# Unused products in two stages' waits, and normalisation statistics taken beside the last attention additions

## The reference

```python
x = x + L0_attn_a(ln(x))   # 16 heads, one shared key and value head, no mask
x = x + L0_ffn(ln(x))      # one 128x128 product, both sides quantised to a 6-bit grid per block of 32
x = x + L0_attn_b(ln(x))   # 16 heads of 64, causal
x = x + L0_ffn(ln(x))
x = x + L1_attn_a(ln(x))   # causal, keys and values from a latent of 32 columns
x = x + L1_ffn(ln(x))      # 8 experts, top 2 by softmax router, plus a shared expert
x = x + L1_attn_b(ln(x))   # causal, with biases
x = x + L1_ffn(ln(x))
```

## Time and profile before

| | us |
|---|---|
| median of 3 runs | 2551.67 |
| lowest, highest | 2545.71, 2552.09 |
| profiled execution | 2546.37 |
| its span, first to last instruction | 2544.7 |
| norm stage, from its first to its last work | 1370.3 to 1408.0 |
| latent attention | 1408.8 to 1791.1 |
| first expert stage's head, to the first gate product | 1792.0 to 1805.1 |
| second expert stage's head, to the first gate product | 2461.1 to 2474.2 |

### The profile page before, as it was taken

One profiled execution on the slowest core, in us unless ns is written; L12 is line 12 of the kernel. 1 busy time (PEld: TensorE's weight loads), 2 busy tenths in 40 slices (PEclk: granted clock), 3 DMA queues, 4 the chain that ended last, 5 costly groups with the idle time before them and its releaser, 6 DMA issues. The chain is left out here.

```text
span 2544.7 us, 48765 instructions
## 1 busy us (share of the span) xinstructions
PE 2449.8 (96%) x20081; PEld 1284.8 (50%) x20081; DVE 1509.0 (59%) x2063; ACT 1216.4 (48%) x1827; POOL 1246.4 (49%) x812
## 2 busy tenths in 40 slices
PE   7999999999999999999997999999989999999989
PEld 4444444444444455545554666666554555455545
DVE  5666656786555664556654567675554555555544
ACT  4544445544545555455542345445334554455541
POOL 4877778777766564555544000000015555555530
PEclk9999999999999999999997899999999999999999
DMA  3000000000000000000001100000000000000000
GB/s 85 1 1 1 1 1 1 1 1 1 1 1 1 1 1 1 1 1 1 1 1 23 35 3 3 3 3 3 1 1 1 1 1 1 1 1 1 1 1 17
DMA packets 18657, 13.04 MB, mean 5 GB/s; under 512 B 3074, under 2 KB 17795, under 8 KB 18308
## 3 DMA queue, kind: packets, MB, share of 16 engines
q1 hardware_dynamic: 18436, 9.92, 1.5%
HBM read 8.87 MB, written 1.05 MB: 4 GB/s over the span
## 5 line engine op out<-in xcount | busy, mean ns | idle before, releaser
L1542 POOL TENSOR_TENSOR sums<-sums,p 128x1024 f32<-128x1024 f32 (+3 forms) x384 | 817.7, 2129 | 370.5 <-PE ps L1169 326.4
L1364 DVE TENSOR_REDUCE half_max<-ps 128x2 f32<-128x1024 f32 (+3 forms) x384 | 442.1, 1153 | 382.3 <-PE ps L1148 344.1
L1261 ACT ACTIVATE p<-ps 128x1024 f32<-128x1024 f32 (+3 forms) x384 | 347.7, 916 | 229.8 <-PE ps L1125 170.4
L1122 PE MATMUL ps<-q,k 64*128 64x512 f32 (+3 forms) x1792 | 428.1, 556 | 0.0
L880 POOL TENSOR_TENSOR sums<-sums,p 128x1024 f32<-128x1024 f32 (+3 forms) x160 | 277.4, 1733 | 187.4 <-PE ps L627 171.1
L1169 PE MATMUL ps<-p,v 128*64 128x512 f32 (+3 forms) x1536 | 338.5, 555 | 0.0
L1125 PE MATMUL ps<-max_row,pick 64*128 64x512 f32 (+3 forms) x896 | 326.3, 725 | 0.0
L779 DVE TENSOR_REDUCE half_max<-ps 128x2 f32<-128x1024 f32 (+3 forms) x128 | 130.1, 1019 | 154.8 <-PE ps L606 121.4
L1148 PE MATMUL ps<-k_near,q_near 64*128 64x512 f32 (+2 forms) x896 | 195.8, 434 | 21.6 <-DVE half_max L1364 19.6
L1785 ACT ACTIVATE p<-ps 128x2048 f32<-128x2048 f32 (+1 forms) x80 | 136.5, 1707 | 163.0 <-PE ps L1681 91.5
L1148 PEld LDWEIGHTS ps<-k_near,q_near 64*128 64x128 f32 x896 | 84.6, 186 | 224.4 <-issue 124.8
(11 more groups left out here) (290 smaller groups left out, 3955.2 us busy)
## 6 DMA issues: line engine op xcount, KB each, us to landing
q_w<-in_wq SPq DMA_DIRECT2D x3, 512.0 KB, 5.4
o_w<-in_wo SPq DMA_DIRECT2D x3, 512.0 KB, 7.7
x<-in_x SPq DMA_DIRECT2D x4, 256.0 KB, 3.8
k_w<-in_wk SPq DMA_DIRECT2D x2, 512.0 KB, 6.8
v_w<-in_wv SPq DMA_DIRECT2D x2, 512.0 KB, 7.5
out<-x SPq DMA_DIRECT2D x4, 256.0 KB, 2.3
p<-in_wq_t SPq DMA_DIRECT2D x1, 512.0 KB, 5.2
p<-in_w_out SPq DMA_DIRECT2D x1, 512.0 KB, 7.2
```

The costliest lines, as they stand in the source:

```text
L1122: nc.tensor.matmul(out[:, head, 0:width], a.k[rows, owner(i) % 3, k * P:(k + 1) * P], a.q[rows, i % 3, s * BANK + lo:(s + 1) * BANK], star ...
L1261: act.activation(probabilities(g)[:, :, lo:BANK], score[g % 2][:, :, 0:BANK - lo], ACT.Exp)\
L1364: last = v.tensor_reduce(out, chunk_ps(c)[:, :, 0:hi - lo], AX.X, ALU.max, negate=True)
L1542: pool.tensor_tensor(sums, sums, probabilities(g)[:, :, lo:BANK], ALU.add).then_inc(summed, 1)
```

## The change

Unused products on TensorE: 60 (`2 * WARM`) at the norm stage's start, before the wait for the weight loads; 30 after the wait for the copied weights; the 30 that stood there before keep their place. In latent attention 15 (`WARM // 2`) stand before chunk 0, at step -6. They are 128x128 products of the identity. At the head of both expert stages the six unused products of 512 columns become four.

Statistics: `m.stats` is now one buffer that outlives the phases. In latent and in biased attention, DVE measures the tiles that it has just added to, for the last two items (i >= ITEMS - B), after a wait for its own addition. These are the last additions into each tile. The expert stages no longer measure at their head. The measuring at the end of the first expert stage, for the layernorm behind it, uses the same buffer.

```diff
--- before.py
+++ after.py
@@ -324,6 +324,12 @@
                     last = nc.tensor.transpose(m.ps[:, 4 + g, t * P:(t + 1) * P], xn[:, g * TPG + t, :], m.ident[:])
                 last.then_inc(turned, 1)
 
+            def keep_busy(times):
+
+                for _ in range(times):
+                    nc.tensor.matmul(m.ps[:, 4, 0:P], m.ident[:], m.ident[:], start=True, stop=True)
+
+            keep_busy(2 * WARM)
             pe.wait_ge(latent_in, 4 * 16)
             for h in range(H):
                 last = nc.tensor.matmul(m.ps[:, 0, h * LATENT:(h + 1) * LATENT], wq_t[:, h, :], k_up_t[:, h, :],
@@ -335,6 +341,7 @@
                                         start=True, stop=True)
             last.then_inc(latent_mm, 1)
             pe.wait_ge(latent_copied, 2)
+            keep_busy(WARM)
             if linear:
                 for pair in groups[::2]:
                     for g in (pair, pair + 1):
@@ -348,8 +355,7 @@
                             last = nc.tensor.matmul(m.ps[:, g, t * P:(t + 1) * P], m.xn_t[:, at:at + P],
                                                     m.ffn_wt[:], start=False, stop=t == TPG - 1)
                         last.then_inc(product, 1)
-                for n in range(WARM):
-                    nc.tensor.matmul(m.ps[:, 0, 0:P], m.ident[:], m.ident[:], start=True, stop=True)
+                keep_busy(WARM)
             for g in groups:
                 pe.wait_ge(normed[g % 2], normed_by(int(linear), g))
                 turn(g)
@@ -826,6 +832,10 @@
                 at = i % B * QT + s * TPG
                 x = m.x[:, at:at + TPG, :]
                 v.tensor_tensor(x, x, small.rearrange("p (t d) -> p t d", d=D), ALU.add).then_inc(small_out, 1)
+                if i >= ITEMS - B:
+                    dve.wait_ge(small_out, n + 1)
+                    for t in range(at, at + TPG):
+                        v.bn_stats(m.stats[:, t, :], m.x[:, t, :])
 
             if biased:
                 v.tensor_scalar(a.qk_bias[:, :, 0:1], a.qk_bias[:, :, 0:1], SCALE, None, ALU.mult)\
@@ -1764,6 +1774,9 @@
 
             for g in range(FIRST, END):
                 ahead, behind = chunks_at(g)
+                if 0 in ahead:
+                    for _ in range(WARM // 2):
+                        nc.tensor.matmul(score[:, 0, 0:P], m.ident[:], m.ident[:], start=True, stop=True)
                 for c in ahead:
                     chunk(c)
                 if 0 <= g < TOTAL:
@@ -1862,6 +1875,10 @@
                 at = i % B * (S // P) + 2 * s
                 x = m.x[:, at:at + 2, :]
                 v.tensor_tensor(x, x, small[:, 0:QW].rearrange("p (t d) -> p t d", d=D), ALU.add).then_inc(small_out, 1)
+                if i >= ITEMS - B:
+                    dve.wait_ge(small_out, n + 1)
+                    for t in (at, at + 1):
+                        v.bn_stats(m.stats[:, t, :], m.x[:, t, :])
 
             v.memset(a.neg_max[:], 0.0).then_inc(cleared, 1)
             dve.wait_ge(cleared, 1)
@@ -1928,7 +1945,7 @@
         gated, upped, spread = sem("gated"), sem("upped"), sem("spread")
         silued, hidden, downed, summed_out = sem("silued"), sem("hidden"), sem("downed"), sem("summed_out")
         first_mul, coef_low, stored = sem("first_mul"), sem("coef_low"), sem("stored")
-        stats, mv = sb("stats", [P, TILES, 6]), sb("mv", [P, TILES, 2])
+        stats, mv = m.stats, sb("mv", [P, TILES, 2])
         var, rstd, shift = (sb(name, [P, TILES]) for name in ("var", "rstd", "shift"))
         logit, prob, coef, rank = (sb(x, [P, TILES, EXPERTS]) for x in ("logit", "prob", "coef", "rank"))
         red = sb("red", [P, TILES])
@@ -2035,7 +2052,7 @@
                 for _ in range(times):
                     nc.tensor.matmul(m.ps[:, bank, :], m.ident[:], m.gate[:, 0:BANK], start=True, stop=True)
 
-            keep_busy(0, 6)
+            keep_busy(0, 4)
             turn(0, 0)
             for g in range(1, GROUPS):
                 turn(0, g)
@@ -2179,8 +2196,6 @@
                 x = m.x[:, g * TPG:(g + 1) * TPG, :]
                 v.tensor_tensor(x, x, m.ps[:, 6, :].rearrange("p (t d) -> p t d", d=D), ALU.add).then_inc(summed_out, 1)
 
-            for g in range(GROUPS):
-                measure(g)
             gather(0, TILES)
             invert(1, 0, TILES)
             for g in range(GROUPS):
@@ -2250,6 +2265,7 @@
         m.ps = ctx.enter_context(nc.psum_tensor("ps", [P, 8, BANK], F32))
         m.x = sb("x", [P, TILES, D])
         m.xn_t = sb("xn_t", [P, T])
+        m.stats = sb("x_stats", [P, TILES, 6])
         m.ident = sb("ident", [P, P])
         m.earlier = sb("earlier", [P, EXPERTS, EXPERTS])
         m.spread = sb("spread_of", [LOW + EXPERTS, EXPERTS * ED], F32R)
```

## The result

Over 20 runs the changed kernel has a median of 2556.96 us (2549.42 to 2564.57), the kernel before, over its 20, 2547.1 us (2543.04 to 2558.29). The ratio over all these runs is 1.0031, 95% interval [1.002, 1.0043] (the two medians alone would give 1.0039): slower by 0.31%, where 0.26% was forecast. The profiled execution has a span of 2551.2 us, 6.5 more than before; the forecast's sum was 6.8. Much of that agreement is luck between its terms, as the stages show.

A forecast was written before the change was run, and what follows sets the result against it. TensorE, busy 96% of the span, was taken as the bound, with the last-arriving engine deciding each edited stretch. 7.7 + 0.4 + 0.6 + 0.55 - 1.72 + 0.95 - 1.72 = +6.8 us on median 2551.67 gave 2558.4, range 2549 to 2564.

The forecast's parts named there:

- main term: Norm stage: the added unused products outlast their waits, making its last turn 7.7 us later.
- L335 in under 4 us: Norm stage: first weight products (L329 before the change) this short would show the forecast wrong and the clock staying high.
- latent attention's opening at full clock past its value products: Start of latent attention: clock still at 1.00 after the value products would show the forecast wrong.
- Norm stage: Second norm stage with 60 and 30 added products: last turn +7.7 us, from +3.5 to +9.8.
- the step that chose between the ends: Norm stage: clock taken as gone 2.5 us into L329, giving +7.7 between +3.5 and +9.8 us.
- the latent row: Profile row where the clock was lost about 2 us after latent attention's K=32 products began, taken as nearest for L329.
- The rule on weight loads: Norm stage rival, chance 0.05: loads take no less time at high clock, 2 us more, 2560.5 us.
- High clock carried: Rival, chance 0.20: clock stays high from the norm stage's first wait well into latent attention, total -1.0, 2550.7 us.
- Latent opening: Latent attention's 15 products: first chunk about 1.9 us late, 1.5 back from high clock, +0.4, from -2.6 to +1.9.
- Statistics: Measuring moved into both attentions: stalls 0.6 us in latent attention, exposed at the ends +0.55 and +0.95 us.
- Expert heads: Both expert stages: four unused products in place of six end 1.72 us sooner, so -1.72 each, nothing more.
- the rival with 0.15: Lighter expert heads leave the clock low when gate products start, 1.7 us each: total +10.2, 2561.9 us; chance 0.15.

The follow-up runs named there:

- c_stats: Kernel before with only the statistics moved beside the last additions, six unused products kept at the expert heads: ratio 1.0014 to the kernel before.
- l_sized: Changed kernel with 30, 15 and 22 unused products in the norm stage in place of 60, 30 and 30: ratio 0.9993 to the kernel before.
- i_best: Kernel before with norm-stage blocks of 30, 15 and 22 unused products and the 15 of latent attention's opening: ratio 0.9985 to the kernel before.
- d_heads: Kernel before with statistics moved and four unused products at the expert heads, norm stage and latent opening untouched: ratio 1.0002 to the kernel before.
- e_first: Kernel before with 30 unused products before the norm stage's weight loads, none after the copies, closing 30 kept: ratio 1.0006 to the kernel before.
- f_fit: Kernel before with only the norm stage's blocks changed, to 30, 15 and 22 unused products: ratio 0.9994 to the kernel before.
- b_latent: Kernel before with only the 15 unused products before latent attention's first chunk: ratio 1.0018 to the kernel before.
- a2_norm: Kernel before with only the norm stage's 60 and 30 unused products added, run a second time: ratio 1.0033 to the kernel before.

## Why the prediction was right, point by point

The total came out as forecast, and so did its main term: products that outlast a wait are paid. Two of the prediction's own signs of being wrong came true as well, L335 in under 4 us and latent attention's opening at full clock past its value products (done at 1425.9, clock lost at 1428.5). The terms behind them were off, and in opposite directions.

- **Norm stage, +7.7 forecast, +5.24 measured.** The first block's time, its 6.4 us past the wait, and the halving of L329 were right (15.3, 6.3 and 3.75 us). So were the FFN products at the high clock. Wrong was the step that chose between the ends: by the latent row I let the clock go 2.5 us into L329 (that row has 2.0), at 1.1 us for L329 and 1.0 for L334. In the eight kernels with a first block it fell 4.3 to 5.5 us after the first weight product, at their end: 0.6 to 0.7 us after the last in the four with 60 or 90 products, 0.1 to 0.7 us before it in the four with 30. So neither the second block nor the pause before it is what the fall follows; what stands before it each time are the small weight products. The 2.1 us foreseen for the clock's return came as 1.8 (8.51 us for the second block, 6.7 for as many products at full clock). Without the terms of 1.1 and 1.0 my sum is 3.5 + 1.8 = 5.3.
- **The rule on weight loads.** L335 in 3.75 us and the router's loads before show that loads follow the granted clock here: 0.22 us for each of L329's records at 0.50, 0.12 at 1.00. The Trainium skill, "TensorE: Matmul & The Clock Gate", LDWEIGHTS, has one price for a load, its columns over 1.2 GHz. For the 128 columns of these loads that is an estimate of 0.107 us each, 3.4 us for 32, if a record is one such load. So the page's price lies near what was measured at the full clock (3.64 us), and not near the 6.90 us at the half clock. The prediction read it the other way round, as keeping the 7.03 us. The measurement decides.
- **High clock carried, the rival with 0.20.** Its sign "L335 in under 4 us" came true, and the clock did last 9.1 us after the start of the first chunk (2.0 before). But the whole didn't come out at -1.0: the second block still lost the clock, and the heads didn't gain. I had tied three things to one condition.
- **Latent opening, +0.4 forecast, -1.96 measured.** The delay of 1.9 was right to 0.02 us. The return was 3.9 and not 1.5: the first chunks, the value products and the second q and k products all ran at the high clock.
- **Statistics.** Latent attention after its first scores: +0.85 in the change, +0.48 to +0.90 in the five kernels with moved statistics (0.6 forecast for stalls). Where the clock's spells lie alike, the stalls are 0.5 (c_stats) and 0.7 (l_sized less i_best); the rest isn't separated from the clock. Exposed: the first expert stage starts 0.50 us later behind the last addition (0.55), the second 0.89 (0.95).
- **Expert heads, -1.72 each forecast.** The turn came 2.0 us and 1.3 us sooner against the stage's start, since the grant came at another point of the block (3.9 and 5.2 us into it, 4.4 and 4.3 before). Right also that nothing more could come of DVE's 3.6 us. Wrong as a net: behind the turn +2.8 and +1.1 were lost to the low clock at the gate products, so the heads netted +0.8 and -0.1 without the exposed statistics. I had this as the rival with 0.15, at 1.7 a head; d_heads and l_sized repeat the net to 0.2 us. At the first head the spell goes with the four products; at the second, six products lose the clock too when it is granted as late. So its price depends on where the grant falls in the block, which the forecast had at 4.4 us everywhere.
- **The total.** +6.8 forecast, +6.5 in the profiles. Norm and latent attention came out 4.6 us better than forecast (+4.1 for +8.7), the expert stages 4.2 worse (+2.3 for -1.9); the two misses nearly cancel.

## What to carry to other kernels

Unused products are worth their time only as far as they end before what the wait waits for: work out the end at the low and at the high clock, and size them for the low one, since past that point each is paid whole (6.75 us for 30). What a high clock wins can be spent at the next wait: e_first's 30 products fit, and its last turn is still 0.21 us later, while in f_fit, which also fills the wait for DVE and closes with 22, it is 4.6 us earlier. The 15 products of the latent opening cost 1.9 us of delay and won 3.9, yet alone they didn't make the kernel faster (b_latent, 1.0018). And work taken off an engine that doesn't arrive last wins nothing: look for the last arrival first, here PE's own fill.

## What the runs showed that I had not expected

- The start of the norm stage, behind 1370 us of untouched code, lay between -3.0 and +4.5 us of the first profile in twelve kernels, and this goes with how much of it is at the low clock: one spell lasts from 26.5 to 43.6 us in a2_norm (+4.41), from 35.1 to 42.0 in the kernel before.
- PE busy for 13.5 of 13.5 us in latent attention's steady part at a granted clock of 0.50 (b_latent), more than 60 us into the phase. From there to the phase's last 3 us no other kernel had a low spell longer than 3.4 us.
- The clock fell within 0.2 us of the start of a block of dense products, at 1391.0 in the changed kernel, after 16.9 us at 1.00 with PE busy 16.42. In e_first it fell in the same part of the stage, with no block behind it: what came before the fall were the small weight products.
